# Reordering three in-order engine programs of a two-layer transformer kernel: an earlier second low part of z and first residual on the vector engine, a later input normalisation on the scalar engine

## The reference, cut to what matters

```python
# layer 0
y = layernorm(x, ln1) * (1 + gamma1) + beta1
x = x + (attention(y) @ proj_w + proj_b) * alpha1        # softmax attention
z = layernorm(x, ln2) * (1 + gamma2) + beta2
x = x + (gelu(z @ fc1_w + fc1_b) @ fc2_w + fc2_b) * alpha2
# layer 1: the same form; scale and shift from ada weights, rotary q and k,
# masked scores, and no alpha gates
```

## Time and profile before

| what | value |
|---|---|
| median of 3 runs | 1976.14 us |
| lowest, highest | 1975.19, 1976.7 us |
| profiled execution | 1976.43 us |
| span of its instructions | 1974.6 us |
| mean granted TensorE clock | 0.984 |
| PE busy | 1813.7 us, 92% of the span |
| ACT busy | 1314.2 us, 67% |
| DVE busy | 1238.8 us, 63% |
| POOL busy | 850.4 us, 43% |
| DMA | 199.84 MB, mean 101 GB/s |

### The profile page before, as it was taken

How to read it: one execution, slowest core, us unless ns; L and a number is a source line. 1 busy time by engine, 2 the same in 40 slices (tenths; PEclk the granted TensorE clock), 3 DMA queues, 4 the chain that set the end, 5 groups by cost and what they waited for, 6 DMA issues and landing times.

```text
span 1974.6 us, 41731 instructions
## 1 busy us (share of the span) xinstructions
PE 1813.7 (92%) x12623; PEld 1642.7 (83%) x12623; DVE 1238.8 (63%) x2973; ACT 1314.2 (67%) x2315; POOL 850.4 (43%) x1036
## 2 busy tenths in 40 slices
PE   4679999999999999999898999999999999999997
PEld 4668888888888888888787889888988888888885
DVE  5657556766655666765666567666566766665651
ACT  3446776676677677677666666676776676677663
POOL 2123333333333334333444555555555455556533
PEclk7889999999999999999999999999999999999999
DMA  6454333444433444433343233333323333322320
GB/s 166 111 124 127 80 98 101 124 115 122 109 90 98 107 117 117 127 93 92 110 141 101 59 103 96 94 102 107 85 78 108 92 94 101 105 82 84 94 63 32
DMA packets 330275, 199.84 MB, mean 101 GB/s; under 512 B 160994, under 2 KB 314596, under 8 KB 330212
## 3 DMA queue, kind: packets, MB, share of 16 engines
q1 hardware_dynamic: 330212, 199.06, 37.6%
HBM read 80.98 MB, written 17.33 MB: 50 GB/s over the span
## 4 chain that ended last, share of the span: by engine, by line
PE 58%; issue 15%; ACT 6%; DVE 6%; SPq 6%; POOL 5%; DMA 4%; POOLq 0%; ACTq 0%; DVEq 0%
PE D L886 15%; PE A L886 11%; PE C L886 10%; PE B L886 8%; PE B L1036 7%; PE B L1022 4%; POOL h_lo L551 3%; DMA x_res<-in_x 3%; ACT x_in L683 2%; SPq L321 2%; SPq L418 2%; ACT v_blocks L735 2%; PE A L1008 1%; ACT hact L740 1%; PE E L1047 1%
## 5 line engine op out<-in xcount | busy, mean ns | idle before, releaser
L551 POOL TENSOR_TENSOR h_lo<-hact,h_hi 128x512 fp32r<-128x512 f32 x256 | 330.3, 1290 | 340.4 <-ACT h_hi L745 332.4
L886 PE MATMUL D<-wgt_hi,h_hi 128*128 128x256 f32 x1024 | 302.8, 296 | 33.0 <-POOL h_lo L551 26.6
L886 PE MATMUL D<-wgt_lo,h_hi 128*128 128x256 f32 x1024 | 290.6, 284 | 0.0
L886 PE MATMUL D<-wgt_hi,h_lo 128*128 128x256 f32 x1024 | 290.5, 284 | 0.0
L740 ACT ACTIVATE hact<-C,b_col 128x512 f32<-128x512 f32 x256 | 176.3, 689 | 146.0 <-PE C L886 143.8
L886 PE MATMUL A<-k_pad,q_pad 128*128 128x256 f32 x1536 | 259.9, 296 | 13.9 <-DVE exps L1341 6.8
L1036 PE MATMUL B<-v_blocks,probs_turned 128*128 128x68 f32 x2048 | 254.1, 271 | 0.0
L1036 PEld LDWEIGHTS B<-v_blocks,probs_turned 128*128 128x128 f32 x2048 | 248.5, 192 | 5.6 <-ACT probs_turned L754 2.6
L754 ACT COPY probs_turned<-B 128x512 f32<-128x512 f32 x256 | 147.8, 585 | 154.7 <-PE B L1022 154.5
L1335 DVE TENSOR_REDUCE mx<-A 128x8 f32<-128x512 f32 x256 | 174.1, 680 | 116.1 <-PE A L1008 61.0
L886 PE MATMUL C<-z_hi,wgt_hi 128*128 128x512 f32 x512 | 213.6, 417 | 29.9 <-ACT hact L740 27.8
(11 more groups left out here) (138 smaller groups left out, 4224.7 us busy)
## 6 DMA issues: line engine op xcount, KB each, us to landing
k_pad<-k_flat SPq DMA_DIRECT2D x512, 64.0 KB, 2.0
q_pad<-q_flat SPq DMA_DIRECT2D x256, 128.0 KB, 2.3
gates<-gates SPq DMA_DIRECT2D x64, 256.0 KB, 4.4
x_bias<-x_bias SPq DMA_DIRECT2D x32, 512.0 KB, 3.4
rotation<-rotation SPq DMA_DIRECT2D x256, 64.0 KB, 1.9
x_in<-in_x SPq DMA_DIRECT2D x16, 512.0 KB, 3.9
gates<-gated_bias SPq DMA_DIRECT2D x32, 256.0 KB, 4.8
x_res<-in_x SPq DMA_DIRECT2D x16, 512.0 KB, 4.3
```

Source lines behind the costliest of these rows:

```text
L551: pool.tensor_tensor(hb[1][:, m % 2, :], hact[:, m % 2, :], hb[0][:, m % 2, :].bitcast(F32), ALU.subtract).then_inc(h_lo, 1)
L886: ins = nc.tensor.matmul(dst, l, r, start=first_start and n == 0, stop=last_stop and n == len(todo) - 1, **kw)
```

## The change

On ACT, `hidden(u-1, 6)` and `hidden_high(u-1, 6)` move ahead of `first_norm(u+2)` and the two copies of columns. On DVE, `z_low(u-1, 1)` moves ahead: in layer 0 behind the first `gate_output`, in layer 1 behind the first `output`. And `residual(u, b, 0)` moves ahead of `subtract(u, 2, 1)`. No instruction is added or taken away.

```diff
@@ ACT, end of step
                 if a is not None:
                     values(u + 1, 1)
+                if c is not None:
+                    hidden(u - 1, c, 6)
+                    hidden_high(u - 1, 6)
                 if n is not None:
                     first_norm(u + 2)
                     first_columns(u + 2, n)
                 if b is not None:
                     second_columns(u, b)
-                if c is not None:
-                    hidden(u - 1, c, 6)
-                    hidden_high(u - 1, 6)
@@ DVE, middle of step
                     z_shift(u - 1, 1)
                 if p == 0:
                     gate_output(u - 2, 0)
+                if p == 1:
+                    output(u - 2, p, 0)
+                if c is not None:
+                    z_low(u - 1, 1)
+                if p == 0:
                     gate_output(u - 2, 1)
+                    output(u - 2, p, 0)
                 if p is not None:
-                    output(u - 2, p, 0)
                     output(u - 2, p, 1)
-                if c is not None:
-                    z_low(u - 1, 1)
                 if b is not None:
                     reciprocals(u, 1, 0)
@@ DVE, first residual
                 if b == 0:
                     gate_heads(u, 0)
                 if b is not None:
+                    residual(u, b, 0)
                     subtract(u, 2, 1)
-                    residual(u, b, 0)
                     second_statistics(u, 0)
```

More of the change, by code:

```diff
@@ L1443, in step @@
                     gate_output(u - 2, 0)
-                    gate_output(u - 2, 1)
-                if p is not None:
+                if p == 1:
                     output(u - 2, p, 0)
-                    output(u - 2, p, 1)
                 if c is not None:
                     z_low(u - 1, 1)
+                if p == 0:
+                    gate_output(u - 2, 1)
+                    output(u - 2, p, 0)
+                if p is not None:
+                    output(u - 2, p, 1)
                 if b is not None:
```

## The result

The changed kernel takes 1927.09 us (median of 4 runs, 1925.46 to 1930.19) against 1975.75 us (4 runs) for the kernel before on the same chip: a ratio of 0.9758, 95% interval 0.9744 to 0.9772. The medians are 48.7 us apart. Forecast was 1934, with a range of 1924 to 1953.

A forecast was written before the change was run, and what follows sets the result against it. PE, busy 92% of the span, was taken as the bound, plus gaps in its stream. Gains of 23.1 us (layer 0), 18.0 (layer 1) and 1.2 (residual-only steps) make 42.3, from 1976.4 to 1934 us, range 1924 to 1953.

The forecast's parts named there:

- ACT's edit: Gelu of chunk 6 ahead of the input's normalisation: PE's wait vanishes, 1.3 us per step in layer 0, 0.77 in layer 1.
- The layer 0 term: Layer 0 gain per step: 1.3 us for the gelu's move; with 0.35 for the residual, 1.65 us.
- The low part of z: Earlier second z_lo on DVE: PE's wait vanishes but moves to the low heads in layer 0; zero gain in both layers.
- The residual: First residual ahead of a subtraction on DVE: 0.35 us per step in layer 0, 0.43 in layer 1.
- the stall of 0.2: DVE waiting for z_hi before the second z_lo: about 0.15 or 0.2 us, counted as lost in layer 0's residual term.
- the lateness at the projection: At `project(u, 1)` in layer 0: DVE late by 0.05 us, leaving 0.35 of a bracket of 0.44.
- The sum: 14 layer 0 steps x 1.65, 15 layer 1 steps x 1.2, three residual-only steps x 0.4: together 42.3 us.
- A: Only ACT's move pays; full DVE takes the residual's gain back at its next low part: 27 us, 1949; chance 0.15.
- B: DVE not the bound in that stretch, all three waits vanish: 2.85 us per layer 0 step, 1918 us; chance 0.05.
- C: ACT's delayed normalisation makes PE late at step start; about 0.5 us per step remain, 1962 us; chance 0.06.
- D: Slower: DVE stalls for z_hi; loses from 1.4 us of stall per step, 1991 us with 1.9; chance 0.05.
- E: Nothing gained: the gaps move to other waits, time stays at 1976 us; chance 0.04.

The follow-up runs named there:

- e1: Only ACT's reorder (gelu and rounded copy of chunk 6 ahead of the input's normalisation) on the kernel before: 1943.11 us, ratio 0.9837.
- e2: Only the earlier second low part of z on DVE, on the kernel before: 1975.31 us, ratio 1.0002.
- e4: ACT's reorder and the earlier first residual, without the earlier low part of z, on the kernel before: 1930.69 us, ratio 0.9770.
- e5: ACT's reorder and the earlier low part of z, without the earlier residual, on the kernel before: 1941.45 us, ratio 0.9829.
- e3: Only the first residual ahead of the subtraction on DVE, on the kernel before: 1961.21 us, ratio 0.9926.
- e6: Changed kernel with the second gate multiplication and second residual addition on DVE cut to one of two groups: 1919.14 us, ratio 0.9714.
- e12: POOL's low part of chunk 5 ahead of the input's reciprocal deviations, on the kernel before: 2004.77 us, ratio 1.0141.

## Why the prediction held, point by point

- **ACT's edit.** The wait vanished whole in both layers, as said: chunk 7's product at 519.67 shifted, against 519.68 by the rows (521.07 less the bracket of 1.23 and the 0.16). Alone it is worth 1.44 and 0.80 per step (e1), against 1.3 and 0.77. The layer 0 term was set too low: `back(u-2, 6)` did gain only 1.24, held by POOL's low part of chunk 6 at its old time, but the exponential came 1.39 earlier, not 1.25 (gelu and copy take the 1.25 that I gave them, but the column copies ended 0.12 sooner before the next gelu, 510.62 to 510.85 against 519.98 to 520.33), and DVE's first gate multiplication came 1.42 earlier (531.76 shifted against 533.18), and 1.40 of it reached the projection.
- **The low part of z.** That it would return nothing in layer 0 and that a wait for ot_lo would stand in its place is what e2, e4 and e5 show. The price of its stall was mis-sized: DVE stalls 0.14 before it (I said 0.15 to 0.2), but from the first gate to the first reciprocal DVE takes 524.31 - 521.16 = 3.15 us, against 3.12 before. The order before had a pause of 0.12 ahead of the outputs that the new order doesn't have. So 0.03 was lost, not 0.2.
- **The residual.** Worth 0.52 and 0.48 alone (e3), against 0.35 and 0.43. Part of the 0.35 was the stall of 0.2 that did not come. Against that, gate and residual stand 0.56 apart (528.15 and 528.71), not 0.47 as in the pair in the earlier trace rows. By the Trainium skill (VectorE: DVE Perf Modes, section The DRAIN you can't avoid) the semaphore between them should cost nothing. Behind the same multiplication an independent instruction starts 0.34 later at one place (532.37 and 532.71), so the dependent pairs, at 0.47 and 0.56, speak against that. But the subtraction, independent too, stood 0.47 behind it before (540.14 and 540.61), so how much of the 0.56 is the dependence is open. I had set that rule against independent instructions that start before their forerunner ends, and this one does not. And I held that the low heads of group 1 "do not move": they come 0.17 earlier relative to the gate (530.66 - 528.15 = 2.51 in the trace after, 2.68 before), so the projection was not in the way of `back(u-1, 0)`, which took the full 0.50. In sum: 0.20 for the stall, 0.05 for the lateness at the projection, less 0.09 for the wider pair, make the 0.35 into 0.51.
- **The sum.** 14 x 1.92 + 15 x 1.25 + 3 x 0.4 = 46.8 us against 42.3 forecast. 3.8 of the 4.5 between them are the layer 0 term, 1.92 for 1.65. The medians differ by 48.7, with 2.8 of uncertainty either way. The counts 14 and 15 take in steps that aren't steady. In the two traces, whose executions are 46.2 apart, twelve steady steps of each layer give 38.3, the four intervals around the change of layer 6.4, what follows the last normalisation of the input 3.7, and the start-up takes 2.2 back.
- **The rivals.** A (the residual's gain taken back) fell to e3. B (DVE not the bound) fell to e2 and e6. C (ACT's delay comes back) fell to e1: at most 0.1 us of it did. D, the slower one, had its stall, at 0.14 instead of the 1.4 that it needed. E (nothing) fell to the result itself.
- **What was to be seen.** Gelu, z_lo and ot_lo went as written. The wait for x_res is 0.30, where about 0.5 was forecast. `back(u-2, 6)` shows no bracket for POOL, though it starts 1.06 behind the scores ahead of it (511.53 and 512.59) instead of 0.80. The stall before z_lo is there but too short for a bracket. One wait more than named stands in layer 0: ot_lo holds PE a second time, 0.36 before the projection of group 1. In layer 1 the residual's wait went, and 0.23 stands at the gelu of chunk 0 instead.

## What to carry to other kernels

A wait on the busiest engine is worth its length only if the engine that ends it has idle time behind that point. Where it is full up to the next meeting, as DVE is here in layer 0, an earlier instruction only moves the gap; what pays is to start the full stretch earlier, to take work out of it, or to move work across a meeting point. And one reorder can turn another from a loss into a gain: before repeating a failed order, ask whose deadline has moved (POOL's deviations behind the low part of chunk 5 cost 30 us under ACT's old order and gain 10 under the new one). To tell effects of a few microseconds apart, compare the steady steps in the trace, which repeat within some 0.1 us and their mean more closely, and not the medians, which take in a start-up and a change of layer that differ by 2 us and more; what an edit does there, the steady steps don't tell.

## What the runs showed of the hardware that was not expected

In e12 PE stands idle 2.06 us for the gelu in each layer 1 step, and in some steps its clock falls right behind that. The same kernel's step from 1309.3 us on, in stretches (columns: stretch, length, then busy time and instructions of PE, its weight load, DVE, ACT and POOL, then the granted clock and DMA):

```profile
1309.30:1315.00 5.70, 3.63 (x18) 3.00 (x18) 0.69 (x3) 3.92 (x9) 3.41 (x8) 0.86 0.12 28
1315.00:1320.00 5.00, 5.00 (x37) 5.00 (x37) 3.64 (x6) 3.75 (x6) 2.96 (x2) 0.82 0.06 13
1320.00:1325.00 5.00, 5.00 (x46) 5.00 (x46) 4.56 (x11) 3.14 (x6) 0.00 (x0) 1.00 0.53 125
```

and PE at the start of it:

```profile
1312.99 0.39 PE L886 MATMUL C<-z_lo,wgt_hi 128*128 128x512 f32 x1
1313.22 0.49 PE L886 MATMUL C<-z_hi,wgt_hi 128*128 128x512 f32 x1
1313.51 0.63 PE L886 MATMUL C<-z_hi,wgt_lo 128*128 128x512 f32 x1
```

The matmuls of 512 columns go from 0.23 us apart to 0.43 (1313.51 to the next at 1313.94), the lower of the two levels, 1.2 instead of 2.4 GHz; the clock is back at 1.00 in the third stretch. Such a step is 60.4 us long against 58.8 for its neighbours with the same wait. Of the twelve steady layer 1 steps five are like that, every second or third one, with a mean granted clock of 0.97; the other seven have 1.00. So in those five the wait of 2.06 us brought 1.6 us more with it. Of the 30 us that e12 lost, some 13 are its longer layer 1 steps (15 x 0.85), 3 the layer 0 steps (14 x 0.22), and 8 the clock in those five (5 x 1.6). The remaining 6 lie mostly in the four intervals around the change of layer (261.1 us against 256.0 before), and their cause was not separated. With PE's waits of up to 1.2 us in the steady steps of the kernel before, the granted clock stood at 1.00 from 200 to 880 us, and so it did in e12's layer 0 with waits of up to 1.5. Why it falls in some of the steps and not in the others was not tested.
